# Hyperbolic self attention in a four-layer perceiver: weights through logarithms and exponentials instead of roots and a wide reciprocal

## What is computed

```python
q_norm_sq = jnp.sum(q * q, axis=-1, keepdims=True)
k_norm_sq = jnp.sum(k * k, axis=-1)[:, :, None, :]
diff_sq = jnp.maximum(q_norm_sq + k_norm_sq - 2.0 * qk, 0.0)
denom = jnp.maximum((1.0 - q_norm_sq) * (1.0 - k_norm_sq), 1e-06)
cosh_arg = jnp.maximum(1.0 + 2.0 * diff_sq / denom, 1.0)
distance = jnp.arccosh(cosh_arg)
attn = jax.nn.softmax(-distance, axis=-1)
out = jnp.einsum('bhnm,bhmd->bhnd', attn, v)
```

## Time and profile before

| what | us |
|---|---|
| median of 3 runs | 7039.74 (7037.17 to 7042.12) |
| the profiled execution, own time | 7040.86 |
| its span | 7039.0 |
| this stage in it | some 485, from 5774 to 6259 |

### The profile page before, as it was taken

How to read it: one execution, slowest core, us unless ns; L and a number is a source line. 1 busy time by engine, 2 the same in 40 slices (tenths; PEclk the granted TensorE clock), 3 DMA queues, 4 the chain that set the end, 5 groups by cost and what they waited for, 6 DMA issues and landing times.

```text
span 7039.0 us, 164882 instructions
## 1 busy us (share of the span) xinstructions
PE 5881.7 (84%) x54018; PEld 4608.7 (65%) x54018; DVE 3909.1 (56%) x12136; ACT 2797.6 (40%) x6611; POOL 1773.5 (25%) x2870
## 2 busy tenths in 40 slices
PE   6888888778779999988888998666679988888888
PEld 4666666777547776666665776664457777766666
DVE  5666665444336665644444665554446659964443
ACT  2444443111224442255544554223435542235555
POOL 3444443000013332200000443550014433310000
PEclk9999999999769998999998999777779998889999
DMA  3000000000001000000000110000001100000000
GB/s 126 17 16 16 16 16 10 0 0 0 0 10 32 28 30 1 0 0 0 0 0 12 34 33 21 0 0 0 0 15 34 32 20 0 0 0 0 0 0 12
DMA packets 43764, 93.43 MB, mean 13 GB/s; under 512 B 7696, under 2 KB 28560, under 8 KB 42640
## 3 DMA queue, kind: packets, MB, share of 16 engines
q1 hardware_dynamic: 43664, 92.09, 4.1%
HBM read 88.92 MB, written 3.15 MB: 13 GB/s over the span
## 4 chain that ended last, share of the span: by engine, by line
issue 44%; PE 39%; DVE 9%; POOL 4%; ACT 2%; DVEq 0%; POOLq 0%; DMA 0%; SPq 0%; ACTq 0%
PE psum_banks L548 5%; PE psum_banks L553 4%; PE psum_banks L613 3%; PE psum_banks L657 3%; PE psum_banks L664 3%; PE psum_banks L617 2%; PE psum_banks L1074 2%; PE psum_banks L1597 2%; PE psum_banks L1573 2%; PE psum_banks L1632 2%; PE psum_banks L1062 1%; POOL scratch L1494 1%; PE psum_banks L1029 1%; DVE scratch L920 1%; DVE scratch L1346 1%
## 5 line engine op out<-in xcount | busy, mean ns | idle before, releaser
L2270 PE MATMUL psum_banks<-w_L_ffn_up,x_normed_T 128*128 128x352 f32 (+3 forms) x2112 | 888.4, 545 | 97.2 <-DVE x_normed_T L2412 63.7
L780 DVE TENSOR_REDUCE scratch<-psum_banks 128x2 f32<-128x514 f32 x768 | 531.5, 692 | 411.1 <-PE psum_banks L548 407.2
L263 POOL TENSOR_TENSOR ln_vareps<-ln_meanvar,ln_eps 128x1 f32<-128x1 f32 x165 | 44.6, 270 | 2789.3 <-DVE ln_meanvar L258 2789.3
L699 ACT ACTIVATE scratch<-psum_banks 128x512 f32<-128x512 f32 x768 | 458.6, 597 | 492.2 <-PE psum_banks L558 486.9
L553 PE MATMUL psum_banks<-scratch 32*128 32x128 f32 x6144 | 640.1, 310 | 8.2 <-ACT scratch L699 6.1
L2308 ACT ACTIVATE scratch<-psum_banks 128x176 f32<-128x176 f32 (+3 forms) x1120 | 398.5, 371 | 622.0 <-PE psum_banks L2270 526.4
L548 PE MATMUL psum_banks<-scratch 32*128 32x257 f32 x3072 | 576.1, 441 | 50.1 <-DVE scratch L781 49.8
L2270 PEld LDWEIGHTS psum_banks<-w_L_ffn_up,x_normed_T 128*128 128x128 f32 x2112 | 418.8, 223 | 233.2 <-issue 112.9
L2256 PE MATMUL psum_banks<-w_L_ffn_down,scratch 128*128 128x128 f32 x4096 | 556.1, 282 | 10.4 <-ACT scratch L2299 10.4
L2248 PEld LDWEIGHTS psum_banks<-consts,scratch 128*128 128x128 f32 x2144 | 277.1, 152 | 438.6 <-issue 271.8
L2452 DVE SCALAR_TENSOR_TENSOR scratch<-scratch,psum_banks 128x176 f32<-128x176 f32 (+2 forms) x704 | 257.9, 374 | 527.6 <-ACT scratch L2308 465.0
(11 more groups left out here) (428 smaller groups left out, 14212.6 us busy)
## 6 DMA issues: line engine op xcount, KB each, us to landing
scratch<-in_ctx SPq DMA_DIRECT2D x99, 514.0 KB, 3.5
scratch<-in_ctx_rows SPq DMA_DIRECT2D x130, 128.0 KB, 2.1
w_L_ffn_up<-in_L_ffn_up SPq DMA_DIRECT2D x1, 2992.0 KB, 10.2
w_L_ffn_down<-in_L_ffn_down SPq DMA_DIRECT2D x1, 2112.0 KB, 12.3
w_L_ffn_up<-in_L_ffn_up SPq DMA_DIRECT2D x1, 2080.0 KB, 8.1
x_tokens<-in_x SPq DMA_DIRECT2D x1, 2048.0 KB, 7.9
scratch<-last_values SPq DMA_DIRECT2D x128, 8.0 KB
out<-x_tokens SPq DMA_DIRECT2D x1, 2048.0 KB, 6.9
```

The source lines that it names most:

```text
L699: act.activation(pT[:, b % 2, 2 * h:2 * h + 2].rearrange("p t c q -> p t (c q)"), W, ACT.Exp).then_inc(exp_ready.sem, 1)
L780: dve.tensor_reduce(parts[:, r.t.odd, 2 * h:2 * h + 2, 0, b], S, X_AXIS, ALU.max, negate=True)
L2270: pe.matmul(U[g % 3][:, 0:fw * halves], k.xnT[:, :], up[:, c0:c0 + fw * halves], start=True, stop=True).then_inc(sg["up_written"].sem, 1)
```

## The change

sqrt(D) becomes exp(0.5 ln(D + 1e-24)), sqrt(D + E) likewise, both on ScalarE. With s = sqrt(D) + sqrt(D + E), the weight is exp(ln E - 2 ln s - max): ScalarE takes ln E and ln s, VectorE joins them, takes the maximum over the 32 keys and subtracts it, and ScalarE takes the exponential, straight into the buffer `pr` that TensorE transposes. The wide reciprocal, the product with E and the quotient by the maximum go. `take_turned` moves behind the first exponential, and one activation table is loaded ahead of the stage.

```diff
@@ scalar engine, one(r)
-            if r.turned:
+            if kind != "L3" and r.turned:
                 take_turned(r.t + -1)
...
                 if r.own:
                     act.wait_ge(d_ready.sem, d_ready.at(r.t, 1))
-                    act.activation(s["sD"], s["D"], ACT.Sqrt)
+                    act.activation(s["sD"], s["D"], ACT.Ln, bias=s["tiny"]).then_inc(log_step.sem, 1)
+                    act.wait_ge(log_step.sem, log_step.at(r.t, 1))
+                    act.activation(s["sD"], s["sD"], ACT.Exp, scale=0.5)
+                if r.turned:
+                    take_turned(r.t + -1)
+                if r.own:
                     act.wait_ge(scores_read.sem, scores_read.at(r.t, 1))
-                    act.activation(s["S"], s["S"], ACT.Sqrt).then_inc(roots.sem, 1)
+                    act.activation(s["S"], s["S"], ACT.Ln).then_inc(log_step.sem, 1)
+                    act.wait_ge(log_step.sem, log_step.at(r.t, 2))
+                    act.activation(s["S"], s["S"], ACT.Exp, scale=0.5).then_inc(roots.sem, 1)
                 if r.after:
                     take_x(r.t + 2)
                 if r.own:
-                    act.wait_ge(root_sum.sem, root_sum.at(r.t, 1))
-                    act.activation(s["S"], s["sD"], ACT.Square).then_inc(squared.sem, 1)
+                    act.activation(s["R"], s["E"], ACT.Ln)
                 if r.turned:
                     take_heads(r.t + -1)
+                if r.own:
+                    act.wait_ge(root_sum.sem, root_sum.at(r.t, 1))
+                    act.activation(s["S"], s["sD"], ACT.Ln).then_inc(logs_ready.sem, 1)
                 if r.after:
                     take_qkv(r.t + 2)
+                if r.own:
+                    act.wait_ge(shifted.sem, shifted.at(r.t, 1))
+                    act.wait_ge(turned_written.sem, turned_written.at(r.t + -1, 1))
+                    act.activation(heads_first(s["pr"]), batches_first(s["R"]), ACT.Exp).then_inc(probs_ready.sem, 1)
...
+        if kind == "L3":
+            act.preload_act_table_set("natural_log_exp_and_others")
+            act.wait_ge(set_up.sem, set_up.at(1))
         plan.run(act, one)
@@ vector engine, one_l3(r)
             heads(r)
             if r.own:
-                dve.wait_ge(squared.sem, squared.at(r.t, 1))
-                link(dve.reciprocal(s["R"], s["S"]), r, "R")
-                link(dve.tensor_tensor(s["R"], s["R"], s["E"], ALU.mult), r, "RE")
-                link(dve.tensor_reduce(s["rs"], s["R"].rearrange("p (u k) -> p u k", k=32), X_AXIS, ALU.max), r, "max")
-                link(dve.reciprocal(s["nm"], s["rs"]), r, "nm")
-                dve.wait_ge(turned_written.sem, turned_written.at(r.t + -1, 1))
-                dve.tensor_tensor(heads_first(s["pr"]), batches_first(s["R"]),
-                                  bc(s["nm"].rearrange("p (b t) -> p b t", b=NB), 3, 32), ALU.mult
-                                  ).then_inc(probs_ready.sem, 1)
+                dve.wait_ge(logs_ready.sem, logs_ready.at(r.t, 1))
+                link(dve.scalar_tensor_tensor(s["R"], s["S"], -2.0, s["R"], ALU.mult, ALU.add), r, "R")
+                link(dve.tensor_reduce(s["nm"], s["R"].rearrange("p (u k) -> p u k", k=32), X_AXIS, ALU.max, negate=True), r,
+                     "max")
+                dve.tensor_tensor(s["R"].rearrange("p (u k) -> p u k", k=32), s["R"].rearrange("p (u k) -> p u k", k=32),
+                                  bc(s["nm"], 2, 32), ALU.add).then_inc(shifted.sem, 1)
...
         if kind == "L3":
+            dve.memset(s["tiny"], 1e-24)
```

More of the change, by code:

```diff
@@ L867, in self_buffers @@
                             "rest": [P, 512], "group": [P, P], "vm": [P, 2, 512], "D": [P, 512], "E": [P, 512],
-                            "S": [P, 512], "sD": [P, 512], "R": [P, 512]}}[kind])
+                            "S": [P, 512], "sD": [P, 512], "R": [P, 512], "tiny": [P, 1]}}[kind])
     return k.scratch(more)
@@ L891, in chain_steps @@
                     + ["rr", "w"] * has.turned + ["stats"] * has.third)
-        return (["E"] * has.own + ["rr", "w"] * has.turned + ["R", "RE", "max", "nm"] * has.own + ["stats"] * has.third)
+        return (["E"] * has.own + ["rr", "w"] * has.turned + ["R", "max"] * has.own + ["stats"] * has.third)
     chain = Steps(k.sig("vector_step"), plan, chain_steps)
@@ L913, in self_attention @@
     else:
-        sq_ready, d_ready, roots, root_sum, squared = (
-            PerTile(k.sig(n), 1) for n in ("squares_ready", "distance_ready", "roots_ready", "root_sum", "root_sum_squared"))
+        sq_ready, d_ready, log_step, roots, root_sum, logs_ready, shifted = (
+            PerTile(k.sig(n), m) for n, m in (("squares_ready", 1), ("distance_ready", 1), ("log_ready", 2), ("roots_ready", 1),
+                                              ("root_sum", 1), ("root_sum_log", 1), ("log_weights_shifted", 1)))
         wq, wk, wv, wo = (k.load(f"L3_attn_W{n}", [P, P]) for n in "qkvo")
```

## The result

The changed kernel takes 7163.05 us (median of 4 runs, 7154.0 to 7166.81) against 7040.93 for the kernel before in its 4 runs: a ratio of 1.0171, with a 95% interval of 1.0155 to 1.0187. It is slower by 122 us, where 92 were forecast. The profiled execution took 7160.9 us.

What follows compares the result with a forecast made beforehand. VectorE was taken to set the 14.34 us round, with TensorE having slack. 30 rounds x (0.4 chain + 2.8 clock) = +96, less 3.6 for round 0 and some 0.6 for a table load: +92, 7132 us, range 7040 to 7200.

Steps and rivals of the forecast that it cites:

- What bounds, and what is taken off: VectorE sets the 14.34 us round; without both reciprocals its own work falls to about 10.6 us a round.
- Where the gain goes: Logarithm behind `take_heads` puts TensorE's scores and heads into VectorE's chain; the 3.75 us taken from VectorE become a wait.
- The chain at a full clock, 14.73: One turn through VectorE, scores, heads, `take_heads` and logarithm takes 14.73 us against 14.34: +0.4 a round.
- The clock, 2.8 us a round: TensorE idles 2.9 us each round, then 6.9 us at half clock; half of that, less slack and waits, costs 2.8.
- The clock stays up: Rival: TensorE's clock falls in a few rounds at most, leaving +0.4 a round: 7048 us, chance 0.14.
- One long stretch: Rival: two half-clock stretches or one long one in most rounds, up to +8.6 a round: 7200 to 7295 us, chance 0.14.
- one stretch in each round: Main case: one half-clock stretch of TensorE per round, 2.1 to 3.8 us a round: 7100 to 7160 us, chance 0.64.
- the way between: Half way to a whole round at half clock on TensorE: +5.5 us a round, 7200 us.
- The wait isn't on the path: Rival: VectorE doesn't wait for heads, TensorE closes the round at 11.9 us: 6963 us; chance 0.08 with smaller gains.
- the signs of being right: VectorE idles 3 to 7 us for the logarithm; rounds 17 to 18 us; clock near 0.8; TensorE's longest wait before transposes.

Runs made afterwards that it cites:

- experiment 2: Kernel before, with only the square of the sum moved behind `take_heads` on ScalarE, no logarithm: 7273.67 us, 1.0331 of the kernel before.
- experiment 7: Kernel of experiment 1, with `take_heads` moved to the end of ScalarE's round, behind `take_qkv` and the closing exponential: 6943.01 us, 0.9851 of the kernel before.
- experiment 9: Kernel before, roots and wide reciprocal kept, with `take_heads` moved to the end of ScalarE's round, behind `take_qkv`: 7038.74 us, 1.0001.
- experiment 4: Changed kernel with twelve unread 128-column matmuls added in TensorE's wait between output(t-1) and turn(t): 7085.23 us, 1.0059 of the kernel before.
- experiment 1: Changed kernel with the logarithm of the sum moved ahead of `take_heads` on ScalarE: 7051.6 us, 1.0017 of the kernel before.
- experiment 6: Kernel of experiment 1 with four 128-column matmuls added between output(t-1) and turn(t): 6984.39 us, 0.9917 of the kernel before.
- Experiment 3: Changed kernel with `take_turned` put back in the first place of ScalarE's round: 7162.17 us, 1.0173 of the kernel before.

## Why the prediction was right, and where its size was off

**What bounds, and what is taken off.** Right. VectorE's busy time in the stage fell by 90 us (421 to 331) and nothing of it reached the round. That is 2.9 a round, and not the 3.6 of the two reciprocals, mainly because L1246, a small product of the head sums, now takes 0.81 us for 0.23, with GpSimd's L926 beside it in the rounds looked at, and this lies in VectorE's wait. The new instruction with a scalar takes 692 ns, as the rows of two tensors did. The activations take 621 to 722 ns for the 630 taken. The figure of 0.72 us that the prediction set beside the row is met by L1168, which has a bias operand; the logarithm on the path (L1186) has none and takes 0.62, so those 3 us were not lost. The table load ran once, ahead of the stage.

**Where the gain goes.** Right, and shown from three sides. The wait stands where it was foretold (6.5 us a round on VectorE for the logarithm behind `take_heads`). The exchange in the kernel before, alone, brings +3.3% (experiment 2). Taking the whole queue from behind `take_heads` brings -1.5% against before (experiment 7), and the same order without logarithms nothing (experiment 9).

**The chain at a full clock, 14.73.** Right: 14.71 or 14.72 in the seven rounds of experiment 4 that had a full clock, or nearly.

**The clock, 2.8 us a round.** This is the term that was mis-sized. The mean round is 18.25, so the clock's share of it is 18.25 - 14.73 = 3.5; in the middle of the stage, where rounds last 18.76, it is 4.0. What was mis-sized in it is the length of the stretch at half the clock: 6.9 us had been carried over from the one round of before that had such a stretch, and a mean of 0.69 over 18.25 us is 11.3 us at 1.2 GHz. One round of TensorE in the changed kernel:

```profile
6020.24 0.86 PE L1053 MATMUL psum_banks<-consts,scratch 128*128 128x128 f32 x4 [2.86 <-ACT scratch L1192]
...
6023.69 0.80 PE L1065 MATMUL psum_banks<-scratch 128*128 128x128 f32 x2
...
6027.95 0.79 PE L994 MATMUL psum_banks<-x_normed_T,w_L_attn_Wq 128*128 128x128 f32 x2 [0.37 <-ACT x_normed_T L1127]
...
6030.67 0.46 PE L1045 MATMUL psum_banks<-scratch 128*128 128x128 f32 x2
6030.96 0.39 PE L1040 MATMUL psum_banks<-scratch 128*128 128x128 f32 x2
...
6033.64 1.06 PE L1075 MATMUL psum_banks<-consts,scratch 128*128 128x128 f32 x8
```

The wait of 2.86 us, then transposes that begin at the full clock and end at half of it (0.86 for 0.66), and half the clock through `values` and `project` (L994, 0.79 for 0.49) into the scores: the pair of L1045 at 6030.67 takes 0.46, the next pair 0.39. From 6020.5 to 6030.8 that is 10.3 us. Each round in the middle of the stage has such a stretch, as forecast (no clock above 0.69 in any of the 27); it is half as long again. Why it is longer than in the kernel before I did not show. In sum 3.9 us a round were lost for 3.2 forecast.

The price of the stretch was off the other way. The prediction took half of its length less 0.65 for what falls on slack and waits. From 11.3 us that would be 5.0, and 3.5 was paid. With the right length and the same rule the forecast would have been 14.34 + 0.4 + 5.0 = 19.7 us a round and some 7198 us. So two errors in this term partly cancel, and the size came out as near as it did partly by luck. What the stretch falls on was not taken apart further.

The Trainium skill ("TensorE: Matmul & The Clock Gate", HAM oscillation) describes a kernel whose waits in each step are longer than this one's 2.86 us, and which pays in each step. The trace here shows the same after the shorter wait, with a clock of 0.69; experiments 1 and 6 show more than that, a clock that falls (to 0.74) without a long wait.

**The rivals.** "The clock stays up" gave 7048; not so, 0.69. "One long stretch" began at 7200. The measured 7163 is between it and the case of one stretch in each round, which was to end at 7160 (its 3.8 a round gives 7150, as 30 x 3.8 - 4 = 110), and 3.9 a round is just above that case too. For the way between, the prediction has +5.5 a round; half way from 3.2 to 8.6 is 5.9, or 7213. "The wait isn't on the path" gave 6963 with a round of 11.9. Once the queue was really open it was 11.33 and 6943, but not by moving the logarithm alone, as I had expected in experiment 1. The slip was to follow one instruction behind `take_heads` and not all three. Of the signs of being right, the wait of VectorE, its releaser and TensorE's longest wait were there; the rounds were to be 17 to 18 us and the clock near 0.8, and they are 18.2 and 19.4 at 0.69.

**`take_turned`.** The prediction said that its move used up TensorE's slack, and that each further delay would cost. Experiment 3 shows that putting it back changes nothing: TensorE comes later than it in these rounds (`values` start at 6023.69 without a wait, and L1123 ended at 6022.58).

## What to carry to other kernels

When an instruction is replaced, compare its place in its engine's queue as well as its duration: ScalarE, which runs its instructions in the order written, held a ready logarithm for 9 us behind a late wait, and with it the engine that had just been relieved. List all the instructions behind the late wait (here three of them mattered), and where the program allows it move the wait to the end of the round before measuring the saving. And when TensorE stops being hidden, don't carry the length of its stretch at half the clock over from the old pattern of waits: here it went from 6.9 to about 11 us. These runs give no rule for it, so measure it.

## What the runs showed of the hardware that I had not expected

Added work on TensorE made the kernel faster twice: twelve matmuls in a wait of 2.86 us took 78 us off, and four matmuls of 0.22 us at a place where TensorE waited 0.41 us took some 70 us off and raised the granted clock from 0.74 to 0.93. Even with the twelve, sixteen of 31 rounds had a stretch at half the clock and lasted 17 us. In the kernel with `take_heads` last, two matmuls of one row less in each round changed neither clock nor time.
